# A new order of the tasks on all five engines in the steady part of a scan, mixture-of-experts and FFN kernel

## The chip, the cores and the metric

One core of one Trainium2 chip. The metric is the device time of one execution in microseconds (us); less is better. The engines are TensorE (PE in the rows, its weight loads PEld), VectorE (DVE), ScalarE (ACT), GpSimd (POOL) and SyncE (SP), which here only issues DMAs.

## The reference, cut to what matters

The input is x of shape (8, 1024, 128). Per sequence there is a selective state space scan with 16 states, then a top-1 mixture of 4 experts, two layer norms, and a gated FFN with a last layer norm:

```python
delta = softplus(x @ Wd + bd);  B = x @ WB + bB;  C = x @ WC + bC;  A = -exp(A_log)
# over time, for each of the 16 states s:
h = clip(exp(min(delta*A[s], 2)) * h + clip(delta*B[s], -2, 2) * x, -100, 100)
y = sum_s(h * C[s]) + x * D_param
routing = softmax(y @ Wr + br); top1
moe = (silu(y @ up_w[e] + up_b[e]) @ down_w[e] + down_b[e]) * top1_w
x1 = layernorm(x + layernorm(y + moe) * ln_w + ln_b)
out = layernorm(x1 + (silu(x1 @ w_gate.T) * (x1 @ w_up.T)) @ w_down.T)
```

## The kernel before

Each of the 8 sequences is a chunk (0 to 7) of 1024 tokens, in two halves of 512. The work of a chunk is cut into tasks; a task is a few instructions of one engine, written in the function `run` of that engine, and it waits by itself on semaphores for what it needs. In which order an engine takes the tasks stands in lists: `PE_ORDER`, `ACT_ORDER`, `DVE_ORDER`, `POOL_ORDER`, `SP_ORDER`. An entry such as `(-1, "up", 3)` is the task `up 3` of the chunk that is one behind the iteration's own. Each list is run through once an iteration, so three chunks are at work at a time: the scan of chunk n, the preparation of chunk n+1, the experts of chunk n-1 and the norms and the FFN of chunk n-2. The `_LAST` lists say in which order the last two chunks' tails are done. Every engine works strictly in its order: a task that waits holds all tasks behind it.

The tasks that matter here:

- Preparation: `z`, `bc` (TensorE) and their copies and `softplus` (ScalarE), `delta`, `dx` (VectorE), `b_turn`, `b_spread h` (TensorE, into PSUM bank T), `b_max`, `bound h` (VectorE, empties bank T), `over`, `flag`: a bound on whether clipping can happen at all. `bc_rest` and `bound_input` are GpSimd's part, `bc_mid`, `widen` and `x_scaled` ScalarE's, `bc_low` VectorE's.
- Scan, for each state s of 0 to 15: `decay s` (ScalarE, L807, exp), `spread s h` (TensorE, L555, B to all partitions into psB), `scan s` (VectorE: two multiplications by dx at L1209, two scans at L1218), `c s` (SP, a DMA of C to all partitions, L458), `prod s` (GpSimd, L1245), `add s` (TensorE, L561, transposed and summed in psY), and `skip` for the D term. Rings limit how far they run apart: 6 decays, 3 states, 3 products, 3 C tiles. `spread s+1` of a half needs `scan s` of this half; `scan s` needs `prod s-3`; `prod s` needs `add s-3`; the DMA `c s` needs `prod s-3`.
- Routing: `y_copy`, `yT_turn`, `yT_copy`, `logits`, `router_shift`, `rank`, `slots`, `router_exp`, `router_pick`, then `scatter 0` to `7` (GpSimd, L1266, indirect DMAs of the tokens to their expert's rows), `rows` (SP, L492), `sort_turn`, `sort_copy`.
- Experts, for 11 blocks k of 128 rows: `weights k` (SP, L486, 514 KB, a ring of 3, so it needs `result k-3`), `up k` (TensorE, L691, banks U0, U1 in turn), `silu k` (ScalarE, L846), `down k` (TensorE, L705, bank T), `result k` (ScalarE, L854); then `store` (SP) and `gather 0` to `7` (GpSimd, L1274).
- Norms and FFN, by halves h: `combine h` (VectorE, L1134), `stats h k` (L1152, L1157), `rstd h k` (GpSimd, L1283 to L1297), `centre h` (L1167), `affine h` (L1181), `x_shift h` (GpSimd, L1306), `norm h k` (ScalarE, L867), `x_turn h` (TensorE, L715, bank D), `x_high`, `x_rest`, `x_low`, `ff_up h 0` to `5` (banks U0, U1), `gate h m` (ScalarE, L904, silu), `ff_mul h m` (VectorE, L1189), `ff_down h`, `ff_part h m` (TensorE, L741, L585, bank D). `norm h 2` empties bank D.

ScalarE holds one table of functions at a time: exp, ln and silu each ask for a table load when another one is in place. Copies and scalings do not.

## Time and profile before

| | |
|---|---|
| time, median of 3 runs | 922.79 us (919.44 to 923.1) |
| span of the profiled execution (first to last instruction) | 920.4 us |
| VectorE busy | 715.4 us (78%) |
| TensorE matmuls busy / weight loads | 640.0 us / 511.3 us |
| GpSimd busy | 566.2 us |
| ScalarE busy | 537.6 us |

The times are of whole executions; for the profiled one there is its span alone, 2.4 us under the median. A busy share is an average over stages. The rows further down show what each engine did in stretches cut at the start of scan 0 of each chunk (33.98, 103.19, 193.43, 292.77, 392.77, 492.17, 590.83 and 690.68 us for chunks 0 to 7; the last scan ends at 788.53). Chunk 3 is the one whose timelines are shown.

### The profile page before, as it was taken

Reading aid. Unit: us, or ns where it says so; the run is one execution under the profiler, and the core shown is the slowest. Engines: PE = TensorE matmul, PEld = TensorE weight load, DVE = VectorE, ACT = ScalarE, POOL = GpSimd, SP = SyncE. Lnnn points to the kernel's source line nnn. Section 1 sums busy time; section 2 is a strip of 40 time slices with the busy share of each in tenths; the row PEclk is TensorE's granted clock in tenths of the full one; section 3 lists DMA queues with packets and bytes.
Section 4 is the critical chain, followed back from the end, with each engine's and each line's share of the span. In section 5 each row is a group of like instructions: output and inputs, shape, how many; then the busy total and the mean of one; then the engine's idle time right before and its main releaser. Section 6 shows DMA issues by size and latency. Waiting matters only on the chain.

```text
span 920.4 us, 14199 instructions
## 1 busy us (share of the span) xinstructions
PE 640.0 (70%) x4263; PEld 511.3 (56%) x4322; DVE 715.4 (78%) x1458; ACT 537.6 (58%) x988; POOL 566.2 (62%) x452
## 2 busy tenths in 40 slices
...
GB/s 102 128 127 115 138 149 148 243 225 189 112 218 237 197 96 190 239 166 153 163 243 202 188 113 219 247 203 85 203 240 138 156 166 247 89 82 154 135 23 24
DMA packets 82087, 149.31 MB, mean 162 GB/s; under 512 B 9404, under 2 KB 51144, under 8 KB 81992
## 3 DMA queue, kind: packets, MB, share of 16 engines
...
q8 instruction: 35, 0.57, 0.3%
...
## 4 chain that ended last, share of the span: by engine, by line
PE 30%; DVE 26%; issue 15%; ACT 15%; DMA 7%; POOL 4%; SPq 1%; another core or an unknown queue 0%; ACTq 0%; DVEq 0%; POOLq 0%
DVE state L1218 12%; DMA weights<-in_w_pack 5%; PE psY L561 4%; PE psU L691 4%; DVE psB L1209 4%; PE psD L585 4%; ACT hid L846 4%; PE psT L705 3%; ACT decay L807 3%; PE psU L732 2%; PE psU L734 2%; DVE bst L1152 2%; PE psB L555 2%; ACT L846 2%; PE psU L619 1%
## 5 line engine op out<-in xcount | busy, mean ns | idle before, releaser
L1245 POOL TENSOR_TENSOR prod<-state,c_wide 128x1024 f32<-128x1024 f32 x128 | 308.4, 2415 | 149.1 <-DVE state L1218 127.3
L1209 DVE TENSOR_TENSOR psB<-dx,psB 128x512 f32<-128x512 f32 x256 | 166.7, 689 | 31.6 <-PE psB L555 13.7
L1218 DVE TENSOR_TENSOR_SCAN state<-decay,state,psB 128x512 f32<-128x512 f32 x128 | 163.8, 1280 | 14.0
L555 PE MATMUL psB<-parts,sel 128*128 128x512 bf16 x198 | 89.5, 466 | 122.4 <-DVE state L1218 121.1
L1218 DVE TENSOR_TENSOR_SCAN state<-decay,psB 128x512 f32<-128x512 f32 x128 | 155.4, 1214 | 3.2 <-ACT decay L807 3.2
L561 PE MATMUL psY<-ident,prod 128*128 128x128 f32 x1024 | 155.0, 305 | 1.1 <-DVE state L1218 0.5
L807 ACT ACTIVATE decay<-delta,a_sb 128x1024 f32<-128x1024 f32 x128 | 142.0, 1141 | 15.7 <-DVE state L1218 7.4
L561 PEld LDWEIGHTS psY<-ident,prod 128*128 128x128 f32 x1024 | 137.5, 159 | 12.3 <-issue 7.9
L555 PEld LDWEIGHTS psB<-parts,sel 128*128 128x128 bf16 x256 | 25.8, 103 | 174.2 <-DVE state L1218 168.1
L846 ACT ACTIVATE hid<-psU,weights 128x128 f32<-128x128 f32 x352 | 99.7, 371 | 39.2 <-PE psU L691 33.7
L691 PE MATMUL psU<-yT_sorted,weights 128*128 128x128 f32 x704 | 96.1, 282 | 19.4 <-DMA weights<-in_w_pack 8.3
L691 PEld LDWEIGHTS psU<-yT_sorted,weights 128*128 128x128 f32 x704 | 86.8, 193 | 29.1 <-issue 15.6
L867 ACT ACTIVATE attn<-attn,shift,rstd 128x128 f32<-128x128 f32 x64 | 26.3, 481 | 124.8 <-POOL shift L1297 124.7
L705 PE MATMUL psT<-weights,hid 128*128 128x128 f32 x704 | 97.5, 281 | 0.0
L1266 POOL DMA_INDIRECT rows_in<-ytok,slot x64 | 66.1, 1033 | 44.2 <-issue 36.1
L705 PEld LDWEIGHTS psT<-weights,hid 128*128 128x128 f32 x704 | 85.8, 192 | 1.8
L1274 POOL DMA_INDIRECT chosen_out<-rows_out,slot x64 | 62.8, 981 | 22.7 <-issue 15.4
L1189 DVE SCALAR_TENSOR_TENSOR hh<-psU,hh 128x512 f32<-128x512 f32 x48 | 31.7, 682 | 40.8 <-PE psU L734 40.3
L854 ACT ACTIVATE result<-psT 128x128 f32<-128x128 f32 x88 | 24.7, 281 | 59.2 <-PE psT L705 57.3
L715 PE MATMUL psD<-ident,attn 128*128 128x128 f32 x60 | 13.3, 362 | 57.0 <-ACT attn L867 55.6
L1283 POOL TENSOR_TENSOR ve<-mv,eps 128x4 f32<-128x4 f32 x48 | 14.1, 294 | 59.8 <-DVE mv L1157 59.3
L585 PE MATMUL psD<-wdn_sb,hh 128*128 128x128 f32 x360 | 44.6, 275 | 0.4
...
## 6 DMA issues: line engine op xcount, KB each, us to landing
c_wide<-c_rows SPq DMA_DIRECT2D x128, 512.0 KB, 5.2
weights<-in_w_pack SPq DMA_DIRECT2D x88, 514.0 KB, 4.2
...
```

What stands on the lines that cost most here:

```text
L555: pe.matmul(tokens(psB, c, h), sel[:, s, :], parts[:, c.n % 2, h * HALF:h * HALF + c.hw], start=True, stop=True).then_inc(b_ready, 1)
L561: mm = pe.matmul(psY[:, j, :], src[:, j * ROWS:(j + 1) * ROWS], ident[:, :], is_transpose=True, start=(first and j % NJ == 0), stop=last, ...
L585: mm = pe.matmul(bank[d][:, cols], hh[:, m, cols], wdn_sb[:, m, :], start=False, stop=(m == NH - 1), skip_group_check=True)
L691: mm = pe.matmul(bank[u][:, f * ROWS:(f + 1) * ROWS], weights[:, q % NW, f * 128:(f + 1) * 128], yT_sorted[:, k * ROWS:(k + 1) * ROWS], st ...
L705: mm = pe.matmul(bank[d][:, 0:D], hid[:, k % 2, f, :], weights[:, q % NW, W_DOWN + f * D:W_DOWN + (f + 1) * D], start=False, stop=(f == NF ...
L807: nc.scalar.activation(decay[:, g % NDECAY, w], delta[:, n % 2, w], ACT.Exp, scale=a_sb[:, s:s + 1]).then_inc(decay_ready, 1)
L846: ins = nc.scalar.activation(hid[:, k % 2, f, :], bank[u][:, f * ROWS:(f + 1) * ROWS], ACT.Silu, bias=weights[:, q % NW, W_UPB + f:W_UPB + ...
L1209: v.tensor_tensor(tokens(psB, c, h), dx[:, n % 2, h * HALF:h * HALF + c.hw], tokens(psB, c, h), ALU.mult).then_inc(inp_ready, 1)
L1218: v.tensor_tensor_scan(state[:, g % NSTATE, t0:t0 + c.hw], decay[:, g % NDECAY, t0:t0 + c.hw], tokens(psB, c, h), before, ALU.mult, ALU.ad ...
L1245: g_.tensor_tensor(prod[:, g % NPROD, w], state[:, g % NSTATE, w], c_wide[:, g % NC, w], ALU.mult).then_inc(prod_ready, 1)
L1266: g_.indirect_dma_start(rows_in, bass.IndirectOffsetOnAxis(slot[:, n % 2, j:j + 1].bitcast(U32), 0), ytok[:, n % 2, j, :], None).then_inc( ...
L1274: g_.indirect_dma_start(chosen_out[:, j, :], None, rows_out, bass.IndirectOffsetOnAxis(slot[:, n % 2, j:j + 1].bitcast(U32), 0)).then_inc( ...
```

## The change

The five `_ORDER` lists and the `_LAST` lists are replaced. No task's own program, no tile and no semaphore is changed, and the tasks are the same ones. The new lists also begin their iteration at another place, which by itself does not change an engine's order; what follows is the order itself, read in the steady part for scan chunk n.

| engine | order before | order after |
|---|---|---|
| TensorE | yT_turn, spread 2, skip, logits | yT_turn, logits, spread 3, rank, skip |
| TensorE | x_turn 0, x_rest 0, add 4, ff_ups, b_turn | add 4, x_turn 0, b_turn, x_rest 0, ff_ups |
| TensorE | sort_turn 0, add 6, up 0, sort_turn 1, spread 10 0, up 1, spread 10 1 | add 7, sort_turn 0, spread 10 0, up 0, sort_turn 1, spread 10 1, up 1 |
| TensorE | spread 13 0, spread 13 1, x_turn 1, up 6, down 5 | spread 13 0, down 4, add 11, x_turn 1, up 6, spread 13 1 |
| TensorE | up 7, ff_up 1 2, spread 14 0, b_spread 1, ff_ups | up 7, b_spread 1, ff_up 1 2, ff_down 1, ff_ups, spread 14 0 |
| ScalarE | z_copy, bc_copy, decay 5, softplus, decays 6, 7, norm 0 1, x_high, decay 8, x_low, decay 9, gates, router_exp, decays 10, 11, 12 | z_copy, decays 4 to 10, bc_copy, decay 11, softplus, decay 12, norm 0 1, x_high, router_exp, x_low, gates, decay 13 |
| ScalarE | silu 9, silu 10, result 9, decay 0, result 10, decay 1 | silu 9, decay 0, result 8, silu 10, result 9, decay 1, result 10 |
| VectorE | combine 1, stats 1 0, centre 1, delta, scan 8; b_max, scan 9 | combine 1, delta, stats 1 0, scan 8; scan 9, b_max, scan 10, centre 1 |
| VectorE | scan 13, dx, bound 1, over, ff_mul 1 0, 1 1, router_pick | router_pick, dx, scan 13, bound 1, ff_mul 1 0, over, 1 1 |
| GpSimd | gathers 0 to 2, prod 1, 3 and 4, prod 2, scatter 0, prod 3, scatter 1, prod 4, x_shift 1, gathers 5 and 6, rstd 0 0, scatter 2, gather 7, scatter 3, rstd 0 1, scatter 4, prod 5, scatters 5 to 7 | gathers 0 to 3, prod 1, prod 2, gathers 4 to 6, prod 3, scatters 0 and 1, prod 4, scatter 2, rstd 0 0, prod 5, scatter 3, gather 7, rstd 0 1, scatters 4 to 7 |
| SP | weights 0, 1, 2, c 5, c 6, c 7, rows, c 8, c 9, c 10, weights 3, x | weights 0, c 5, c 6, weights 1, c 7, weights 2, c 8, rows, c 9, weights 3, c 10 |
| SP | weights 4, 5, c 11, c 12, weights 6, c 13 | weights 4, c 11, weights 5, x, weights 6, c 12, weights 7, c 13 |

The diff, cut to the lines that hold these places:

```diff
@@ -67,70 +67,68 @@
 PE_ORDER = [
-    (-1, "yT_turn"), (0, "spread", 2, 0), (0, "spread", 2, 1), (0, "skip"), (-1, "logits"), (0, "spread", 3, 0),
...
-    (0, "spread", 12, 1), (-1, "up", 5), (0, "add", 10), (-1, "down", 4), (0, "spread", 13, 0), (0, "spread", 13, 1),
-    (-2, "x_turn", 1), (-1, "up", 6), (-1, "down", 5), (-2, "x_rest", 1), (0, "add", 11), (-2, "ff_up", 1, 0),
...
+    (-2, "down", 4), (-1, "add", 11), (-3, "x_turn", 1), (-2, "up", 6), (-1, "spread", 13, 1), (-3, "x_rest", 1),
+    (-2, "down", 5), (-2, "warm"), (-3, "ff_up", 1, 0), (-3, "ff_up", 1, 1), (-2, "down", 6), (-2, "up", 7),
+    (0, "b_spread", 1), (-3, "ff_up", 1, 2), (-3, "ff_down", 1), (-3, "ff_up", 1, 3), (-3, "ff_up", 1, 4),
+    (-1, "spread", 14, 0), (-2, "down", 7), (-3, "ff_up", 1, 5), (-1, "spread", 14, 1), (-2, "up", 8),
...
 ACT_ORDER = [
-    (-2, "silu", 10), (-2, "result", 9), (0, "decay", 0), (-2, "result", 10), (-3, "norm", 1, 2), (0, "decay", 1),
...
-    (0, "decay", 5), (1, "softplus"), (0, "decay", 6), (0, "decay", 7), (-2, "norm", 0, 1), (-2, "x_high", 0),
-    (0, "decay", 8), (-2, "x_low", 0), (0, "decay", 9), (-2, "gate", 0, 0), (-2, "gate", 0, 1), (-2, "gate", 0, 2),
...
+    (-1, "decay", 7), (-1, "decay", 8), (-1, "decay", 9), (-1, "decay", 10), (0, "bc_copy"), (-1, "decay", 11),
+    (0, "softplus"), (-1, "decay", 12), (-3, "norm", 0, 1), (-3, "x_high", 0), (-2, "router_exp"), (-3, "x_low", 0),
+    (-3, "gate", 0, 0), (-3, "gate", 0, 1), (-3, "gate", 0, 2), (-1, "decay", 13), (-2, "sort_copy", 0),
...
+    (-2, "silu", 8), (-2, "silu", 9), (0, "decay", 0), (-2, "result", 8), (-2, "silu", 10), (-2, "result", 9),
+    (0, "decay", 1), (-2, "result", 10), (-3, "norm", 1, 2), (-1, "y_copy"), (0, "decay", 2), (-1, "yT_copy"),
...
 POOL_ORDER = [
-    (-2, "gather", 5), (-2, "gather", 6), (-2, "rstd", 0, 0), (-1, "scatter", 2), (-2, "gather", 7),
-    (-1, "scatter", 3), (-2, "rstd", 0, 1), (-1, "scatter", 4), (0, "prod", 5), (-1, "scatter", 5),
...
+    (-5, "gather", 6), (-3, "prod", 3), (-4, "scatter", 0), (-4, "scatter", 1), (-3, "prod", 4), (-4, "scatter", 2),
+    (-5, "rstd", 0, 0), (-3, "prod", 5), (-4, "scatter", 3), (-5, "gather", 7), (-5, "rstd", 0, 1),
+    (-4, "scatter", 4), (-4, "scatter", 5), (-4, "scatter", 6), (-4, "scatter", 7), (-3, "prod", 6), (-3, "prod", 7),
...
 PE_LAST = [
-    (-1, "ff_up", 0, 3), (-1, "ff_up", 0, 4), (-1, "ff_down", 0), (-1, "ff_up", 0, 5), (-1, "ff_part", 0, 0),
-    (-1, "ff_part", 0, 1), (-1, "ff_part", 0, 2), (-1, "x_turn", 1), (-1, "x_rest", 1), (-1, "ff_up", 1, 0),
+    (-1, "ff_up", 0, 3), (-1, "ff_down", 0), (-1, "ff_up", 0, 4), (-1, "ff_part", 0, 0), (-1, "ff_up", 0, 5),
+    (-1, "x_turn", 1), (-1, "ff_part", 0, 1), (-1, "x_rest", 1), (-1, "ff_part", 0, 2), (-1, "ff_up", 1, 0),
```

## Rows read from the trace of the kernel before

**Rows 1.** The page's first part: busy us, share of the span and instructions of each engine.
```profile
PE 640.0 (70%) x4263; PEld 511.3 (56%) x4322; DVE 715.4 (78%) x1458; ACT 537.6 (58%) x988; POOL 566.2 (62%) x452
```

**Rows 2.** Windows, scan 0 to scan 0: busy PE, PEld, DVE, ACT, POOL; clock; DMA.
```profile
103.19:193.43 90.24, 65.40 (x424) 53.73 (x432) 73.65 (x113) 50.69 (x93) 53.27 (x28) 0.82 0.57 186
193.43:292.77 99.34, 75.23 (x529) 61.49 (x537) 87.96 (x178) 66.67 (x121) 70.87 (x57) 0.86 0.57 186
292.77:392.77 100.00, 75.47 (x530) 61.49 (x538) 88.33 (x179) 68.02 (x125) 70.84 (x57) 0.88 0.58 184
...
590.83:690.68 99.85, 75.00 (x529) 61.40 (x536) 88.04 (x178) 68.08 (x125) 70.84 (x56) 0.88 0.58 187
690.68:788.53 97.85, 71.78 (x504) 60.13 (x512) 81.24 (x163) 54.63 (x111) 64.90 (x54) 0.84 0.53 173
788.53:920.40 131.87, 78.00 (x495) 60.96 (x493) 41.11 (x177) 47.74 (x122) 47.82 (x68) 0.79 0.28 83
```

**Rows 3.** VectorE's waits in chunk 3, 292.77 to 392.77: total us, times, longest.
```profile
DVE holder L1043 <- PE psT L637: 4.9, 2, 4.1
DVE psB L1209 <- PE psB L555: 2.2, 3, 0.9
...
DVE state L1218 <- ACT decay L807: 0.5, 1, 0.5
```

**Rows 4.** The page's costliest groups, one of them: busy us, mean ns, idle before.
```profile
L1218 DVE TENSOR_TENSOR_SCAN state<-decay,state,psB 128x512 f32<-128x512 f32 x128 | 163.8, 1280 | 14.0
```

**Rows 5.** Timeline of VectorE, chunk 3 and (411.96) 4: start us, us, instruction, idle before.
```profile
332.72 3.16 DVE L1134 SCALAR_TENSOR_TENSOR moe<-chosen_out,top_w,ytok 128x128 f32<-128x128 f32 x4
...
339.54 1.29 DVE L1209 TENSOR_TENSOR psB<-dx,psB 128x512 f32<-128x512 f32 x2
...
373.95 1.20 DVE L1030 TENSOR_TENSOR dx<-delta,xT_sb 128x1024 f32<-128x1024 f32 x1
379.27 0.06 DVE L1043 MEMSET holder<- 128x1 f32 x1 [4.11 <-PE psT L637]
...
411.96 1.14 DVE L1134 SCALAR_TENSOR_TENSOR moe<-chosen_out,top_w,ytok 128x128 f32<-128x128 f32 x4
```

**Rows 6.** Timeline of GpSimd in chunk 3: prod 5 and prod 13.
```profile
332.52 2.35 POOL L1245 TENSOR_TENSOR prod<-state,c_wide 128x1024 f32<-128x1024 f32 x1
...
374.12 3.25 POOL L1245 TENSOR_TENSOR prod<-state,c_wide 128x1024 f32<-128x1024 f32 x1 [1.18 <-DVE state L1218]
```

**Rows 7.** Timeline of ScalarE in chunk 3: norm 0 1, gates, norm 0 2.
```profile
331.01 1.65 ACT L867 ACTIVATE attn<-attn,shift,rstd 128x128 f32<-128x128 f32 x4 [12.31 <-POOL shift L1297]
...
338.01 1.28 ACT L904 ACT_TABLE_LOAD   x1
339.31 1.08 ACT L904 ACTIVATE hh<-psU 128x512 f32<-128x512 f32 x2
...
368.32 1.53 ACT L867 ACTIVATE x<-psD,shift,rstd 128x128 f32<-128x128 f32 x4
```

**Rows 8.** Timeline of TensorE's weight loads in chunk 3: up 5, x_turn 1, b_spread 1.
```profile
366.94 0.97 PEld L691 LDWEIGHTS psU<-yT_sorted,weights 128*128 128x128 f32 x8 [1.41 <-DMA weights<-in_w_pack]
...
370.03 0.57 PEld L715 LDWEIGHTS psD<-ident,attn 128*128 128x128 f32 x4
...
378.43 0.43 PEld L637 LDWEIGHTS psT<-identb,bmax 128*128 128x128 bf16 x4
```

**Rows 9.** The page's DMA issues: KB each, median us to landing.
```profile
weights<-in_w_pack SPq DMA_DIRECT2D x88, 514.0 KB, 4.2
```

**Rows 10.** Timeline of GpSimd in the tail: x_shift 1, scatter 2, scatter 7.
```profile
805.26 1.27 POOL L1306 TENSOR_TENSOR xt<-xt,lnb_sb 128x512 f32<-128x512 f32 x1
...
812.66 1.05 POOL L1266 DMA_INDIRECT rows_in<-ytok,slot  x1 [2.28 <-issue]
...
822.74 0.97 POOL L1266 DMA_INDIRECT rows_in<-ytok,slot  x1 [0.30 <-issue]
```

**Rows 11.** Timeline of TensorE in the last chunk's FFN: x_turn 1.
```profile
902.46 0.47 PEld L715 LDWEIGHTS psT<-ident,attn 128*128 128x128 f32 x4
```

More of the change, by code:

```diff
@@ L85 @@
[L85 to L88 removed]
+    (0, "b_spread", 0), (-1, "add", 8), (-1, "spread", 12, 0), (-1, "add", 9), (-3, "ff_part", 0, 2),
@@ new lines @@
+    (-3, "ff_part", 1, 0), (-2, "up", 9), (-3, "ff_part", 1, 1), (-3, "ff_part", 1, 2), (-2, "down", 8),
+    (-1, "spread", 15, 0), (-1, "spread", 15, 1), (-1, "add", 12), (-2, "up", 10), (-2, "down", 9),
+    (0, "spread", 0, 0), (-1, "add", 13), (0, "spread", 0, 1), (-2, "down", 10), (-1, "add", 14), (0, "spread", 1, 0),
+    (-1, "add", 15), (0, "spread", 1, 1), (1, "z"), (0, "spread", 2, 0), (-1, "yT_turn"), (0, "spread", 2, 1),
+    (-1, "logits"), (0, "spread", 3, 0), (0, "spread", 3, 1), (-1, "rank"), (0, "skip"), (0, "spread", 4, 0),
```

94 lines of the change are left out of this document (42 added, 52 removed), and 7 rows, old and new, of the table SP_ORDER.

## The prediction

> **What bounds the kernel now.** I read the busy shares first, then the same shares cut at each chunk's scan 0, then what VectorE waited for within one chunk, and last the timelines of all engines over that chunk. No engine is full over the whole span [rows 1]. Cut by chunk, VectorE is busy 88.3 of 100.0 us in chunk 3 and 88.0 of 99.9 in chunk 6; chunks 2 to 6, five such periods, add up to 497.3 us (193.43 to 690.68). TensorE's weight loads take 61.5 of 100 [rows 2]. So the steady part hangs on VectorE, with about 12 us a chunk in which it does nothing. Of those, 7.6 have a name: 4.9 waiting for `b_spread` ahead of `bound`, 2.2 for `spread`, 0.5 for a decay [rows 3]. The rest (some 4 us) is steps between instructions of 0.03 to 0.26 us; no order removes them all, and I leave 3.3 standing. A `scan` task is two multiplications, 1.29 us together [rows 5], and two scans of 1.28 or a little less [rows 4], which gives 3.8; sixteen take 61 us. VectorE's work is thus one fixed pile. An order can win named waits, one slow row (below), the ramp and the tail, and nothing more.
>
> From here "+40" is 40 us after the chunk's scan 0 starts. Before, a chunk has two halves: to about +50 VectorE runs without a hole, while TensorE, ScalarE and GpSimd have slack (ScalarE idles 12.3 us ahead of the norm at 331.01, +38.2 [rows 7]); from +50 to +100 TensorE is nearly full, VectorE waits for it.
>
> **What the change moves, and what each is worth.** No instruction is added but table loads. Per steady chunk, by engine:
>
> (a) GpSimd: prod 5 goes ahead of scatter 3, gathers 2 to 6 go ahead, both x_shifts go behind prod 12 and 14. Before, prod 5 starts at 332.52, 0.20 us ahead of combine 1 [rows 6]; that combine takes 3.16 us [rows 5] where the one at 411.96 takes 1.14 [rows 5]. In the new order GpSimd by then does rstd 0 1 (it still ends at +38.2) and four scatters; prod 5, free since scan 5 ends at +29.1, is over by +32.6. Combine 1 at +40.0 then costs 1.14: 2.0 us a chunk, on VectorE's path. The Trainium skill, "SBUF — State Buffer", Who interferes with whom, has the rule: a VectorE instruction with two SBUF inputs and a GpSimd one that reads SBUF exclude each other, the first to issue holding out the other. The row agrees; by a rule of shared bandwidth both would stretch, and prod took its usual 2.35.
>
> (b) VectorE: centre 1 goes from before scan 8 to behind scan 10, b_max behind scan 9, dx and router_pick ahead of scan 13. A move within a full stretch costs nothing; it lets scans 8 to 10 and the FFN multiplications start 1.1 us sooner. With (a): scan 8 at +43.7 instead of +46.8 (339.54 [rows 5]).
>
> (c) ScalarE: decays 8 to 12 and softplus move into the 12.3 us hole ahead of norm 0 1 (decay 12 needs scan 6, which ends at +33.8; its end is then +37.5, the norm's start +38.2, so nothing is late). bc_copy waits behind decay 10 and ends at +28; its readers come at +41. Gate 0 0 comes at +44.3 instead of +46.5 (339.31 [rows 7]), since decay 9 no longer stands between x_low and it. router_exp comes before the gates. Silu 0 comes at +52.8 instead of +56.4.
>
> (d) Table loads: exp, ln and silu each need their own. Read off the two lists, a chunk has 8 switches before and 10 after. Six only change their place; the two new ones come from silu 10, which now stands between decays 0 and 1. A switch is 1.28 us, 1.3 to the next start (338.01 to 339.31 [rows 7]), so 2.6 to 2.9 us more of ScalarE per chunk. At the chunk's end: decay 0 done +92.7, silu 10 +95.6, decay 1 +98.4; scan 1 asks for decay 1 at +100.1. Hidden by 1.7 us; if that cover is gone it costs 1 for 1. And decay 0 no longer comes late: 0.5 won [rows 3].
>
> (e) TensorE: add 4 and b_turn come earlier, skip after logits, spreads 10 and 11 ahead of the expert matmuls, b_spread 1 ahead of the last ff_ups. I walked the list on with durations of the rows (up 0.97, b_spread 0.43, x_turn 0.57 [rows 8]; down and add, 9 and 8 weight loads like up's 8, at 1.0 and 0.9; a hand-over between engines at 0.1 to 0.3): bound 0 starts at +65.8 (before: +70.3) with no wait for b_spread, scan 12 at +68.5 (+73.2), norm 0 2 ends at +73.3 (+77.1, from 368.32 plus 1.53 [rows 7]). Then new waits begin. Spread 13's second half now stands behind x_turn 1 and up 6. Weights 6 are asked for when result 3 is out, +69.3, and land 5 us after issue (median 4.2 [rows 9], and a C load joins), so up 6 runs at +75.1, the spread at +76.1, and scan 13 loses 2.0. Bound 1 waits for result 6 (+80.7) and b_spread 1: 2.5 lost, against 4.11 before [rows 5]. The multiplications behind lose 0.9, spreads 11 and 12 together 0.7. VectorE's waits: 6.1 instead of 7.6.
>
> (f) SP: c 10 now stands behind weights 3, c 12 behind weights 6, c 4 behind prod 1, which is behind four gathers. Each waiting DMA holds those behind it. Prod 12 so starts at +76 and ends at +78.4; scan 15 is the first to need it, at +92.4: 14 us of cover. Prod 10: +68.2 against scan 13 at +73.9, 5.7 of cover. And the late c 12 keeps prod 12 off dx (+72.7), which otherwise collide as in (a): before, dx at 373.95 [rows 5] pushed prod 13 to 3.25 us [rows 6]; if prod came first, dx would pay up to 2.3. Cost nothing, range 0 to 2.3.
>
> Sum per chunk: +96.2 by the walk, less the 0.5 of (d) that the first scan no longer waits: 95.7, of which 88.3 - 2.0 is work, 6.1 waits, 3.3 steps. Against 99.45 (497.3 / 5) that is 3.8 us, five times: 19. Bounds of the period: if only (a) holds, 97.4; if (e)'s waits all vanish, 89.6, of which I keep half, 92.6.
>
> **Ramp and tail.** Chunk 1 (90.2 us, VectorE 73.7 busy [rows 2]) waits at scans 9 to 12 for prod 6 and for spreads behind `up`; prod 5 earlier and the spreads ahead give 3.5 (between 0 and 6). Chunk 0 nothing. Chunk 7 (97.85) wins 2.0 from (a) and about 1 more: 3. In the tail, 131.9 us long [rows 2], the chain is slots, scatters 0 to 7, rows, experts. Before, x_shift 1 (1.27) and two gathers (1.3 each) stand in the midst of the scatters and GpSimd sits 2.28 before scatter 2; the last scatter starts at 822.74 [rows 10]. The new order has gathers 5 and 6 done before the slots are ready and x_shift before that: 3.9 less. Whether the 2.28 also go I can't tell; I take 4 (3.8 to 5.9). The experts (some 40 us) I leave as they are. In the last chunk's FFN, x_turn 1 at 902.46 [rows 11] stood behind ff_part 0 0 to 0 2 and now stands behind one of them: 2 (0 to 2.5). Tail: 6.
>
> Total 19 + 3.5 + 3 + 6 = 31.5 off the profiled execution's 920.4, 888.9. The median of the three runs shown, 922.79, lies 2.4 above that span; off the median it is 891.3.
>
> **Rivals.**
> Half the gain: the walk overlooks a wait of 2 to 2.5 us per chunk (dx against a prod, say). For: two of the covers above are under 2 us. Against: dx and prod 12 are 3 us apart. Time: 891.3 + 6 x 2.4 = 906.
> The two new table loads are on the path: 2.9 more per chunk, seven chunks, 891 + 20 = 911. Against: 1.7 us of cover at decay 1. The Trainium skill, "ScalarE: Activation LUTs", What ACT_TABLE_LOAD costs, adds a drain of 1.38 us to the 1.28 of every switch. By it the two extra would be 5.3 us a chunk and the time, my estimate from that page, 928, a little slower than before. The trace shows the next start 1.30 after the load's [rows 7], so no such drain here: 2 in 100, counted with the slower ones.
> Slower: the second half of spread 13, behind x_turn 1. That one waits for norm 0 2; before, both halves stood ahead of it (370.03 [rows 8]), so that the norm's lateness cost VectorE little. Now each us that the norm is later than +73.3 is a us of scan 13. 3.8 us eat the steady gain, from 6.3 on the kernel is slower; at 7.5 (rstd 0 2 stuck behind bound_input, rstd 1 1 and prod 10 because x_scaled is late) a chunk takes 103.2: 922.8 + 5 x 3.75 - 3.5 - 3 - 6 = 929.
> No change: gains in the steady part eaten fully, only some of the tail left: 919.
>
> **Chances.** Forecast 0.68 (its own range 880 to 900); half the gain 0.12; table loads on the path 0.05; no change within 0.5% (4.6 us, about what three runs can tell from nothing) 0.06; slower 0.09. The forecast's own case is 891. Leaving out the slower case, the no-change case and 5 in 100 at the low end: 878 (a period of 92.6 gives 891 - 5 x 3.1 = 876) to 912. Faster 0.85, same 0.06, slower 0.09.
>
> **What would show it.** Right: scan 0 to scan 0 at 95 to 97; combine 1 at 1.14 us in every chunk; 70 table loads instead of 58; a VectorE wait of about 2 us in the midst of scan 13, one of 2.5 before bound 1; the tail's last scatter 16 to 17 us after scatter 0's slots instead of 20. Wrong, if: combine 1 stays at 3.16, dx or centre 1 grows past 1.3, scan 1 waits for decay 1, the gap ahead of bound 1 stays at 4, or prod 12 holds up scan 15.

## The result, and the profile after

The changed kernel takes 911.94 us (median of 4 runs, 910.26 to 914.84) against 922.94 for the kernel before beside it; the ratio is 0.989, 95% interval 0.987 to 0.992. It is faster, by 11 us, where 31.5 were forecast. The profiled execution took 914.84 us, its span is 913.0. One of the eleven executions of the kernel before beside experiments 1, 2, 5 and 8 took 1057.18 us at a granted clock of 0.611 instead of about 0.83; their bracketed median of 924.4 holds it, the ratios leave it out. The page's first part (busy us, share, instructions of each engine):

```profile
PE 656.4 (72%) x4256; PEld 535.3 (59%) x4322; DVE 730.1 (80%) x1458; ACT 553.4 (61%) x1000; POOL 559.5 (61%) x452
```

VectorE does the same 1458 instructions and is busy 14.7 us longer than before [rows 1]. That is the first sign: its work is a fixed pile, so something on it got slower. The same windows as in [rows 2], cut at the new starts of scan 0 (chunks 1, 2, 4, 6, 7 and the tail):

```profile
106.35:191.13 84.78, 61.68 (x423) 51.45 (x431) 73.44 (x113) 52.71 (x92) 52.77 (x28) 0.86 0.59 201
191.13:290.75 99.62, 77.47 (x534) 64.13 (x541) 91.28 (x180) 70.69 (x128) 70.00 (x56) 0.86 0.55 184
...
388.87:488.82 99.95, 78.34 (x528) 64.65 (x537) 91.53 (x179) 70.51 (x127) 69.91 (x56) 0.85 0.57 184
...
586.86:686.98 100.12, 78.61 (x529) 64.67 (x537) 91.61 (x180) 70.76 (x127) 69.97 (x56) 0.85 0.55 184
686.98:787.45 100.47, 72.45 (x491) 61.03 (x500) 84.94 (x163) 53.04 (x107) 64.73 (x54) 0.85 0.53 172
787.45:913.01 125.56, 79.29 (x499) 64.15 (x498) 39.54 (x176) 48.34 (x127) 46.25 (x67) 0.76 0.29 87
```

Chunks 2 to 6 take 495.9 us (191.13 to 686.98) instead of 497.3: the steady part, where 19 were forecast, gave 1.4. VectorE is busy 91.5 in chunk 4, not the 86.3 of the forecast. The waits of VectorE in chunk 4, against those of [rows 3] (total us, times, longest):

```profile
DVE hh L1186 <- PE psU L731: 1.9, 4, 0.8
DVE holder L1040 <- PE psT L634: 1.9, 1, 1.9
DVE psB L1206 <- remote: 1.0, 1, 1.0
DVE psB L1206 <- issue: 0.3, 1, 0.3
```

So the waits did fall, to 5.1 us. Before they were 8.2: the 7.6 that the prediction read from [rows 3], and a row of 0.6 ("remote", ahead of L1209) that isn't among the lines shown there. The forecast was 6.1. What took their place stands in no list of waits; it is a long bar. Timelines of VectorE and GpSimd, chunk 4, from scan 2's end (all lines after the lists are 3 lower than before: L1065 is L1068, L1131 is L1134, L1206 is L1209, L1242 is L1245):

```profile
399.99 0.17 DVE L1060 TENSOR_TENSOR rs<-psT,br_sb 128x32 f32<-128x32 f32 x1
...
400.49 4.34 DVE L1065 TENSOR_TENSOR rs<-rs,rsmall 128x32 f32<-128x32 f32 x1
404.86 0.19 DVE L1069 SCALAR_TENSOR_TENSOR rcode<-rs,rev_sb 128x32 f32<-128x32 f32 x1
...
410.97 3.11 DVE L1131 SCALAR_TENSOR_TENSOR moe<-chosen_out,top_w,ytok 128x128 f32<-128x128 f32 x4
...
433.68 1.17 DVE L1131 SCALAR_TENSOR_TENSOR moe<-chosen_out,top_w,ytok 128x128 f32<-128x128 f32 x4
```

```profile
400.11 4.66 POOL L1242 TENSOR_TENSOR prod<-state,c_wide 128x1024 f32<-128x1024 f32 x2
...
410.80 2.35 POOL L1242 TENSOR_TENSOR prod<-state,c_wide 128x1024 f32<-128x1024 f32 x1 [2.40 <-PE psY L558]
```

The subtraction of `router_shift` works on 128x32 elements and takes 0.19 us when it is alone. Here it starts at 400.49, while prod 1 and prod 2 run back to back from 400.11 to 404.77, and ends at 404.83, just behind them. Combine 1, at 433.68, takes 1.17 us as forecast, but combine 0, at 410.97, starts 0.17 us behind prod 3 and takes 3.11. In the windows of chunks 2 to 7 the whole task `router_shift` takes 5.5 us instead of 1.4 to 1.6; combine 0 is long in four of them (2, 4, 6 and 7), 2.98 to 3.23 us instead of 1.14.

### The profile page after: what moved, and what is told of

Same layout as the page of the kernel before. It is cut to its first block, busy times and chain, and to the rows that moved or that the text cites. A ratio compares the mean times of both kernels' runs of the same rounds, so it can differ in the third digit from the quotient of the medians.

```text
span 913.0 us, 14204 instructions
## 1 busy us (share of the span) xinstructions
PE 656.4 (72%) x4256; PEld 535.3 (59%) x4322; DVE 730.1 (80%) x1458; ACT 553.4 (61%) x1000; POOL 559.5 (61%) x452
## 4 chain that ended last, share of the span: by engine, by line
DVE 35%; PE 25%; issue 18%; ACT 9%; POOL 7%; DMA 3%; SPq 1%; DVEq 1%; ACTq 0%; POOLq 0%; another core or an unknown queue 0%
DVE state L1215 14%; DVE psB L1206 6%; PE psT L702 4%; PE psU L688 3%; PE psU L731 3%; DVE rs L1065 3%; DVE bst L1149 3%; PE psU L729 3%; PE psD L582 2%; ACT hid L843 2%; PE psY L558 2%; POOL prod L1242 2%; DVE attn L1178 2%; ACT x L864 1%; ACT attn L864 1%
## 5 line engine op out<-in xcount | busy, mean ns | idle before, releaser
L1242 POOL TENSOR_TENSOR prod<-state,c_wide 128x1024 f32<-128x1024 f32 x128 | 303.0, 2376 | 160.0 <-DVE state L1215 109.2
L804 ACT ACTIVATE decay<-delta,a_sb 128x1024 f32<-128x1024 f32 x128 | 142.8, 1145 | 108.5 <-DVE state L1215 106.9
L1206 DVE TENSOR_TENSOR psB<-dx,psB 128x512 f32<-128x512 f32 x256 | 166.1, 688 | 20.8 <-remote 10.4
L1215 DVE TENSOR_TENSOR_SCAN state<-decay,state,psB 128x512 f32<-128x512 f32 x128 | 163.8, 1280 | 14.4 <-DVE state L1215 0.5
L552 PE MATMUL psB<-parts,sel 128*128 128x512 bf16 x191 | 86.1, 454 | 121.5 <-DVE state L1215 118.0
L558 PE MATMUL psY<-ident,prod 128*128 128x128 f32 x1024 | 161.6, 313 | 5.6 <-POOL prod L1242 2.6
L558 PEld LDWEIGHTS psY<-ident,prod 128*128 128x128 f32 x1024 | 146.4, 166 | 20.0 <-issue 10.2
L1263 POOL DMA_INDIRECT rows_in<-ytok,slot x64 | 69.5, 1086 | 21.0 <-issue 21.0
L1280 POOL TENSOR_TENSOR ve<-mv,eps 128x4 f32<-128x4 f32 x48 | 9.7, 201 | 71.2 <-DVE mv L1154 70.8
L582 PEld LDWEIGHTS psD<-wdn_sb,hh 128*128 128x128 f32 x360 | 43.5, 192 | 0.2
```

What stands on the lines that cost most here:

```text
L552: pe.matmul(tokens(psB, c, h), sel[:, s, :], parts[:, c.n % 2, h * HALF:h * HALF + c.hw], start=True, stop=True).then_inc(b_ready, 1)
L558: mm = pe.matmul(psY[:, j, :], src[:, j * ROWS:(j + 1) * ROWS], ident[:, :], is_transpose=True, start=(first and j % NJ == 0), stop=last, ...
L582: mm = pe.matmul(bank[d][:, cols], hh[:, m, cols], wdn_sb[:, m, :], start=False, stop=(m == NH - 1), skip_group_check=True)
L804: nc.scalar.activation(decay[:, g % NDECAY, w], delta[:, n % 2, w], ACT.Exp, scale=a_sb[:, s:s + 1]).then_inc(decay_ready, 1)
L1206: v.tensor_tensor(tokens(psB, c, h), dx[:, n % 2, h * HALF:h * HALF + c.hw], tokens(psB, c, h), ALU.mult).then_inc(inp_ready, 1)
L1215: v.tensor_tensor_scan(state[:, g % NSTATE, t0:t0 + c.hw], decay[:, g % NDECAY, t0:t0 + c.hw], tokens(psB, c, h), before, ALU.mult, ALU.ad ...
```

## The experiments

Times are medians, in brackets beside the kernel before on the same chip; "caught" means that a VectorE instruction was stretched beside a GpSimd product. Chunk n is always the window from scan 0 of chunk n on. The diffs are cut, some within a line, to the tasks that moved; experiment 2's and 3's leave out the lines of the semaphores and of the other operands.

**1. One task moved: prod 1 away from router_shift.**

```diff
-    (-5, "gather", 2), (-5, "gather", 3), (-3, "prod", 1), (-3, "prod", 2), (-5, "gather", 4),
+    (-5, "gather", 2), (-5, "gather", 3), (-3, "prod", 2), (-5, "gather", 4),
...
-    (-3, "prod", 14), (-4, "x_shift", 1), (-5, "rstd", 1, 2), (-3, "prod", 15), (-2, "prod", 0), (-4, "gather", 0),
-    (-4, "gather", 1),
+    (-3, "prod", 14), (-4, "x_shift", 1), (-5, "rstd", 1, 2), (-3, "prod", 15), (-2, "prod", 0), (-4, "gather", 0),
+    (-2, "prod", 1), (-4, "gather", 1),
```

> The changed kernel with one task moved: prod 1 goes from behind gather 3 to behind gather 0, so that two gathers and more lie between prod 1 and prod 2. Theory of the lock: in the changed kernel the subtraction inside router_shift (two inputs in SBUF) takes 4.3 us instead of 0.19 because GpSimd runs prod 1 and prod 2 back to back beside it. Here it should take about 0.2, and combine 0, which met prod 3 in half of the chunks at 3.1 us, should take 1.14 everywhere; six chunks times 4.15 plus about 7 for combine 0 would be 31, of which I expect 20 to 28: 884 to 892, period from scan 0 to scan 0 94 to 96. Rival (the steady part is held elsewhere: TensorE, the late half of spread 13, the two table loads): the subtraction gets short but the period stays above 97.5 and the time above 905, the time going to longer waits ahead of bound and in the midst of scan 13.

Measured: 887.3 us (924.4), ratio 0.961 (0.958 to 0.965). Timeline of VectorE, then of GpSimd, chunk 4:

```profile
391.27 0.17 DVE L1060 TENSOR_TENSOR rs<-psT,br_sb 128x32 f32<-128x32 f32 x1
...
391.76 0.19 DVE L1065 TENSOR_TENSOR rs<-rs,rsmall 128x32 f32<-128x32 f32 x1
```

```profile
387.75 2.35 POOL L1242 TENSOR_TENSOR prod<-state,c_wide 128x1024 f32<-128x1024 f32 x1
...
393.75 2.37 POOL L1242 TENSOR_TENSOR prod<-state,c_wide 128x1024 f32<-128x1024 f32 x1
```

Prod 1 (387.75) is over before the task, prod 2 (393.75) starts after it, and the subtraction takes 0.19. Combine 0 takes 1.14 to 1.16 in every chunk, too. The windows of chunks 3 and 4 show periods of 94.2 and 93.9 with VectorE busy 85.4:

```profile
285.90:380.10 94.20, 77.27 (x529) 64.47 (x537) 85.41 (x179) 70.61 (x127) 69.98 (x56) 0.89 0.60 196
380.10:474.00 93.90, 78.22 (x529) 64.94 (x537) 85.47 (x179) 70.55 (x127) 70.11 (x56) 0.87 0.59 196
```

In the changed kernel the five steady chunks took 25.4 us more than here (495.9 against 470.5), and the two tasks account for 26.5: `router_shift` took 5.45 to 5.54 instead of 1.35 to 1.38 in each of the five, 20.7 together, and combine 0 1.84, 1.97 and 1.98 more in three of them, 5.8. VectorE's waits in chunk 4 are, row for row, those shown above, so the time didn't go to other waits: the rival falls. The profiled execution is the fastest of six here (879.66); the whole spans differ by 35.1 (913.0 and 877.9), the medians by 24.6.

**2. The subtraction's input moved to PSUM, orders kept.** The addition writes bank T back, and maximum and subtraction read it there.

```diff
-                    v.tensor_tensor(rs[:, j, :], rs[:, j, :], wide(rsmall[:, 0, j], c.tiles, E), ALU.subtract
+                    v.tensor_tensor(rs[:, j, :], psr, wide(rsmall[:, 0, j], c.tiles, E), ALU.subtract
```

> The changed kernel with all its orders, but router_shift keeps its biased logits in PSUM: the addition writes bank T back, maximum and subtraction read bank T, so that the subtraction has one input in SBUF and one in PSUM. Bank T comes free three small instructions later (0.6 us). Theory of the lock: prod 1 and prod 2 still run back to back beside it, and the subtraction takes about 0.2 us all the same; the time falls by 15 to 25 to 887 to 897 (combine 0 may still meet prod 3). Rival (the subtraction is slow because VectorE's and GpSimd's traffic compete for SBUF, or because it waits for something else, such as the result of the maximum): it still takes over 1 us, and the time stays within 5 us of 912.

Measured: 911.3 us (924.4), ratio 0.988 (0.983 to 0.992): no gain over the changed kernel. Timeline of VectorE, chunk 4:

```profile
401.01 0.19 DVE L1066 TENSOR_TENSOR rs<-psT,rsmall 128x32 f32<-128x32 f32 x1
401.35 4.00 DVE L1071 SCALAR_TENSOR_TENSOR rcode<-rs,rev_sb 128x32 f32<-128x32 f32 x1
```

I had the price right for the instruction and wrong for the task: the subtraction, in the midst of the products (400.63 to 405.29), now takes 0.19, and the next one with two inputs in SBUF takes 4.00.

**3. All of router_shift with at most one input in SBUF, orders kept.** Biased logits, shifted ones and codes stay in bank T; a copy to rs is added for ScalarE.

```diff
+                    v.tensor_copy(rs[:, j, :], psr).then_inc(router_steps, 2)
-                    v.scalar_tensor_tensor(out=rcode[:, j, :], in0=rs[:, j, :], scalar=0.0,
+                    v.scalar_tensor_tensor(out=psc, in0=psr, scalar=0.0,
...
-                    v.tensor_tensor(chosen[:, j, :], rcode[:, j, :], wide(rsmall[:, 1, j], c.tiles, E), ALU.is_equal
+                    v.tensor_tensor(chosen[:, j, :], psc, wide(rsmall[:, 1, j], c.tiles, E), ALU.is_equal
```

> The changed kernel with all its orders; now every instruction of router_shift between the addition and chosen has at most one input in SBUF: the biased logits, the shifted ones and the codes stay in bank T, one small copy to rs is added for ScalarE. In the run that moved only the subtraction's input, the subtraction took 0.19 us and the next instruction with two SBUF inputs (rcode) took 4.00: the hold-up went to the next one in line. Theory of the lock: with none left, prod 1 and prod 2 still run back to back (4.66 us together) and router_shift takes about 1.6 us; nothing else holds, so the time falls by 20 to 28 to 884 to 892, the same as with prod 1 moved. Rival (VectorE is slowed by any GpSimd work beside it, or the later release of bank T costs TensorE as much): 900 or more, with some instruction of router_shift still above 1 us.

Measured: 899.6 us (921.8), ratio 0.976 (0.973 to 0.979). Timelines of GpSimd and VectorE, chunk 4:

```profile
397.42 4.67 POOL L1248 TENSOR_TENSOR prod<-state,c_wide 128x1024 f32<-128x1024 f32 x2
```

```profile
397.72 0.20 DVE L1067 TENSOR_TENSOR psT<-psT,rsmall 128x32 f32<-128x32 f32 x1
...
398.13 0.19 DVE L1072 SCALAR_TENSOR_TENSOR psT<-psT,rev_sb 128x32 f32<-128x32 f32 x1
...
398.58 0.19 DVE L1078 TENSOR_TENSOR chosen<-psT,rsmall 128x32 bf16<-128x32 f32 x1
399.22 1.29 DVE L1212 TENSOR_TENSOR psB<-dx,psB 128x512 f32<-128x512 f32 x2 [0.45 <-DVE chosen L1078]
...
404.66 3.96 DVE L1137 SCALAR_TENSOR_TENSOR moe<-chosen_out,top_w,ytok 128x128 f32<-128x128 f32 x4
```

The two products run over the whole task, and none of its instructions takes more than 0.20 us. The orders and the arithmetic are kept (a small copy and three semaphore steps come on top), so VectorE isn't slowed by GpSimd's work as such. The time, 899.6, misses my 884 to 892, and fell by half of what I expected, because combine 0 now comes to stand beside prod 3 (3.96 here), and a hand-over of 0.45 was added.

**4. A pause between the two products:** gather 4 goes in between.

```diff
-    (-5, "gather", 2), (-5, "gather", 3), (-3, "prod", 1), (-3, "prod", 2), (-5, "gather", 4),
+    (-5, "gather", 2), (-5, "gather", 3), (-3, "prod", 1), (-5, "gather", 4), (-3, "prod", 2),
```

> The changed kernel with gather 4 moved in between prod 1 and prod 2, so that about 1.2 us in which GpSimd reads no SBUF by its vector units lie between the two products; prod 1 still starts where router_shift's subtraction comes. Theory 1 (the subtraction is held as long as GpSimd goes from one such instruction straight to the next, and gets in at the first pause): it takes 2.0 to 2.3 us instead of 4.34, router_shift 3.2 to 3.5, 2.3 a chunk less, six chunks: 914 - 12 = 898 to 902. Theory 2 (held for the number of products that GpSimd has queued, or until its queue is empty): still over 4 us, 908 to 914. Theory 3 (a fixed wait of about 4 us): the same as theory 2 in time, with exactly 4.3.

Measured: 911.4 us (920.5), ratio 0.992 (0.989 to 0.995). Timelines of VectorE and GpSimd, chunk 4:

```profile
401.39 2.05 DVE L1065 TENSOR_TENSOR rs<-rs,rsmall 128x32 f32<-128x32 f32 x1
...
403.92 3.04 DVE L1075 TENSOR_TENSOR chosen<-rcode,rsmall 128x32 bf16<-128x32 f32 x1
```

```profile
401.02 2.36 POOL L1242 TENSOR_TENSOR prod<-state,c_wide 128x1024 f32<-128x1024 f32 x1
403.54 0.98 POOL L1271 DMA_INDIRECT chosen_out<-rows_out,slot  x1 [0.16 <-issue]
404.55 2.35 POOL L1242 TENSOR_TENSOR prod<-state,c_wide 128x1024 f32<-128x1024 f32 x1
```

Theory 1 holds for the instruction: held by prod 1 alone, the subtraction takes 2.05 us and gets in at the pause. But the time didn't follow, because the task's last instruction has two inputs in SBUF as well; it is ready at 403.92 and ends at 406.96, behind prod 2 (404.55 to 406.90). Its start is put 0.6 us ahead of prod 2's, in the midst of gather 4, and so it is in each of chunks 2 to 7 here.

The gather isn't what holds: over all runs 933 starts of such instructions (router_shift's three, combine, centre and affine) fall within a gather or scatter that has no instruction right behind it, and all take their usual 0.19 to 0.21 or 0.32 to 0.35 us. Of the 79 that start within one with a product right behind it, 29 are held through that product. Their starts lie 0.16 to 0.71 us ahead of the product's; of the 50 that aren't held, 45 start 0.71 to 1.06 ahead. So it isn't enough to start first by the trace: within some 0.7 us the product mostly wins. Whether it took the ports before its start in the trace, or the start of VectorE's instruction isn't its grant, stays open.

**5. My part (a) alone, in the kernel before:** prod 5 ahead of scatter 3.

```diff
-    (-1, "scatter", 3), (-2, "rstd", 0, 1), (-1, "scatter", 4), (0, "prod", 5), (-1, "scatter", 5),
+    (0, "prod", 5), (-1, "scatter", 3), (-2, "rstd", 0, 1), (-1, "scatter", 4), (-1, "scatter", 5),
```

> The kernel before with one task moved: prod 5 goes from behind scatter 4 to ahead of scatter 3. My part (a) alone. By my prediction combine 1 falls from 3.16 to 1.14 in the chunks where it was long, 2.0 us a chunk, 7 chunks: 909 to 913. Rival (VectorE's slack is decided behind +50 by TensorE, and what is won at combine 1 is waited away at bound 0 or at spreads 11 to 13): combine 1 gets short, the waits for b_spread and spread grow by as much, and the time stays above 918.

Measured: 939.1 us (924.4), ratio 1.017 (1.012 to 1.021). Neither theory: the time lies above the rival's 918, but not by the rival's mechanism. Timelines of VectorE and GpSimd, chunk 3:

```profile
326.74 3.97 DVE L1181 SCALAR_TENSOR_TENSOR attn<-moe,rstd,xt 128x128 f32<-128x128 f32 x4
...
335.79 1.12 DVE L1134 SCALAR_TENSOR_TENSOR moe<-chosen_out,top_w,ytok 128x128 f32<-128x128 f32 x4
...
342.33 1.30 DVE L1209 TENSOR_TENSOR psB<-dx,psB 128x512 f32<-128x512 f32 x2 [1.65 <-PE psB L555]
```

```profile
327.68 2.35 POOL L1245 TENSOR_TENSOR prod<-state,c_wide 128x1024 f32<-128x1024 f32 x1
```

Combine 1 is short, but prod 5 now falls on `affine 0`, which takes 3.97 us instead of 1.12. And the 2.0 won behind it aren't kept: affine 0 feeds norm 0 1, the gates and, through TensorE's order, spread 8, for which VectorE now waits 1.65. The period of chunk 3 grows by as much as affine 0, 2.8 (102.8 instead of 100.0).

**6. GpSimd's new steady list in the kernel before, all else as before.** Its core:

```diff
-    (-2, "gather", 0), (-2, "gather", 1), (-2, "gather", 2), (0, "prod", 1), (-2, "gather", 3), (-2, "gather", 4),
-    (0, "prod", 2), (-1, "scatter", 0), (0, "prod", 3), (-1, "scatter", 1), (0, "prod", 4), (-2, "x_shift", 1),
...
+    (-5, "gather", 2), (-5, "gather", 3), (-3, "prod", 1), (-3, "prod", 2), (-5, "gather", 4), (-5, "gather", 5),
+    (-5, "gather", 6), (-3, "prod", 3), (-4, "scatter", 0), (-4, "scatter", 1), (-3, "prod", 4), (-4, "scatter", 2),
```

> The kernel before with GpSimd's steady list of the changed kernel, all other lists as before. By the lock theory prod 1 and prod 2 now run back to back just when scan 2 ends and router_shift begins: its subtraction grows from 0.2 to 0.5 us to about 4.3, six chunks, plus 24. Combine 1 gets short (2.0 us a chunk), but the run with prod 5 moved alone showed that lateness of norm 0 1 is passed on whole and that scan 8 then waits for its spread; so I count little for it: 935 to 948. Rival, the sum of my prediction (combine 1 counts in full, and four less in the scatters): 905 to 915.

Measured: 970.1 us (921.8), ratio 1.052 (1.048 to 1.055), beyond even my 935 to 948. Timelines of VectorE and GpSimd, chunk 3:

```profile
352.75 6.34 DVE L1167 SCALAR_TENSOR_TENSOR moe<-moe,mv,lnw_sb 128x128 f32<-128x128 f32 x4
```

```profile
353.72 4.69 POOL L1245 TENSOR_TENSOR prod<-state,c_wide 128x1024 f32<-128x1024 f32 x2
```

In chunk 3 `router_shift` takes 5.22 (before 1.63), combine 0 1.81 (1.15), centre 0 3.20 (1.12), combine 1 1.17 (3.16), and centre 1, caught by prod 6 and prod 7 in a row, 6.34 (1.14): 3.6 + 0.7 + 2.1 - 2.0 + 5.2 = 9.6, of which shorter waits give back 0.7 (7.5 instead of 8.2): the period is 108.5 instead of 100.0. The list that is good with the new VectorE order costs 48 us with the old one. My sum had treated (a) as a property of GpSimd's list.

**7. Part (a) undone inside experiment 1:** prod 5 back behind scatter 4.

```diff
-    (-5, "rstd", 0, 0), (-3, "prod", 5), (-4, "scatter", 3), (-5, "gather", 7), (-5, "rstd", 0, 1),
-    (-4, "scatter", 4), (-4, "scatter", 5),
+    (-5, "rstd", 0, 0), (-4, "scatter", 3), (-5, "gather", 7), (-5, "rstd", 0, 1),
+    (-4, "scatter", 4), (-3, "prod", 5), (-4, "scatter", 5),
```

> The changed kernel with prod 1 behind gather 0 (887.3 us) and prod 5 put back behind scatter 4, which undoes my part (a) inside the new order. Prod 5 then starts about 0.2 us ahead of combine 1, which should take 3.0 to 3.2 us again instead of 1.14. Theory A (part (a) as predicted, 2.0 us a chunk on VectorE's path): 899 to 902. Theory B (VectorE waits 1.24 us ahead of ff_mul 0 0 for ScalarE's gates, which hang on affine 0 and norm 0 1, not on combine 1; the delay is taken up by that wait and the 0.1 to 0.3 behind it): 0.5 us a chunk, 889 to 893.

Measured: 893.6 us (921.8), ratio 0.971 (0.968 to 0.973), between the theories. Timeline of VectorE, chunk 3:

```profile
326.27 3.17 DVE L1131 SCALAR_TENSOR_TENSOR moe<-chosen_out,top_w,ytok 128x128 f32<-128x128 f32 x4
...
335.54 1.26 DVE L1186 SCALAR_TENSOR_TENSOR hh<-psU,hh 128x512 f32<-128x512 f32 x2
```

Set beside experiment 1 from scan 0 on, combine 1 ends 2.1 us later, scan 9 0.6 later (the wait ahead of `ff_mul 0 0` took up the rest), then centre 1 is caught for 0.5 and bound 1 waits 0.3 longer: 1.35 at the end of the chunk. Part (a) is worth 1.35 a chunk in this order, not 2.0.

**8. Two table loads fewer:** silu 10 ahead of decay 0 again, in the changed kernel.

```diff
-    (-2, "silu", 8), (-2, "silu", 9), (0, "decay", 0), (-2, "result", 8), (-2, "silu", 10), (-2, "result", 9),
+    (-2, "silu", 8), (-2, "silu", 9), (-2, "silu", 10), (0, "decay", 0), (-2, "result", 8), (-2, "result", 9),
```

> The changed kernel with silu 10 put back ahead of decay 0, and so two table loads fewer a chunk (58 in all instead of 70). My prediction: the two loads are hidden, the time stays within 3 us of 912. Rival (they are on the path, 2.9 us a chunk): 892 to 900. Decay 0 comes some 3 us later here, so up to 0.5 a chunk may be lost at scan 0.

Measured: 946.5 us (924.4), ratio 1.027 (1.022 to 1.031), 35 us slower than the changed kernel and outside both theories. Timelines of ScalarE and VectorE, end of chunk 3:

```profile
396.29 1.14 ACT L843 ACTIVATE hid<-psU,weights 128x128 f32<-128x128 f32 x4 [3.85 <-PE psU L688]
...
398.74 1.15 ACT L804 ACTIVATE decay<-delta,a_sb 128x1024 f32<-128x1024 f32 x1
399.80 0.26 ACT L851 ACTIVATE result<-psT 128x128 f32<-128x128 f32 x1
```

```profile
401.54 0.69 DVE L1206 TENSOR_TENSOR psB<-dx,psB 128x512 f32<-128x512 f32 x1 [2.92 <-PE psB L552]
403.48 0.70 DVE L1206 TENSOR_TENSOR psB<-dx,psB 128x512 f32<-128x512 f32 x1 [1.25 <-PE psB L552]
```

Silu 10 waits 3.85 us for up 10, which the new TensorE order has put late. Behind it stand decay 0 and result 8; down 9 needs result 8, and spread 0 stands behind down 9. VectorE waits 4.2 us for it. So the two extra loads buy something I had priced at 0.5: with this TensorE order decay 0 and result 8 can't stand behind silu 10. For the loads themselves the sign is in the changed kernel, where VectorE waits for decay 1 in no chunk; no run takes them out alone.

**9. Spread 13 in one piece, in experiment 1.**

```diff
-    (-2, "down", 4), (-1, "add", 11), (-3, "x_turn", 1), (-2, "up", 6), (-1, "spread", 13, 1), (-3, "x_rest", 1),
+    (-2, "down", 4), (-1, "spread", 13, 1), (-1, "add", 11), (-3, "x_turn", 1), (-2, "up", 6), (-3, "x_rest", 1),
```

> The changed kernel with prod 1 behind gather 0 (887.3 us in its run) and one more task moved: on TensorE the second half of spread 13 goes from behind up 6 to directly behind down 4, so that it no longer waits for x_turn 1 and up 6. My prediction's rival put a price of 1 for 1 on that place. Theory A (bound 1 waits for b_spread 1 behind up 7, so what scan 13 no longer waits, about 1.0 us a chunk, bound 1 waits longer): within 2 us of 887. Theory B (the wait in scan 13 is on the path): 6 to 8 us less, 879 to 881.

Measured: 886.1 us (921.8), ratio 0.962 (0.959 to 0.964), the same as experiment 1. VectorE's wait for b_spread 1 in chunk 3:

```profile
DVE holder L1040 <- PE psT L634: 2.8, 1, 2.8
```

The wait in the midst of scan 13 (0.8 in chunk 3 of experiment 1, 1.0 in chunk 4) is gone, bound 1 waits 2.8 instead of 1.9, and the multiplications behind it 1.9 instead of 2.4. Chunks 2 to 6 take 470.3 us, against 470.5. Theory A.

**10. That wait attacked: b_spread 1 ahead of down 6, in experiment 9.**

```diff
-    (-2, "down", 5), (-2, "warm"), (-3, "ff_up", 1, 0), (-3, "ff_up", 1, 1), (-2, "down", 6), (-2, "up", 7),
-    (0, "b_spread", 1), (-3, "ff_up", 1, 2),
+    (-2, "down", 5), (-2, "warm"), (-3, "ff_up", 1, 0), (-3, "ff_up", 1, 1), (0, "b_spread", 1), (-2, "down", 6),
+    (-2, "up", 7), (-3, "ff_up", 1, 2),
```

> The fastest order so far (prod 1 behind gather 0, spread 13 unparted, 886.1 us) with b_spread 1 moved on TensorE from behind up 7 to ahead of down 6. Bound 1 now waits 2.9 us a chunk for it. Theory A (that wait is on the path and can be had): 2 us a chunk less, six or seven chunks, 872 to 876. Theory B (TensorE is the bound between +70 and +90: down 6 now waits until bound 1 has emptied bank T, and VectorE waits as much longer for ff_up, for spread 14 or for decay 0): within 3 us of 886, or slower.

Measured: 900.5 us (920.5), ratio 0.977 (0.974 to 0.980). Timelines of VectorE and of TensorE's weight loads, chunk 3:

```profile
371.19 0.06 DVE L1040 MEMSET holder<- 128x1 f32 x1 [0.86 <-PE psT L634]
...
376.81 0.69 DVE L1186 SCALAR_TENSOR_TENSOR hh<-psU,hh 128x512 f32<-128x512 f32 x1 [4.27 <-PE psU L731]
```

```profile
372.59 0.10 PEld L699 LDWEIGHTS psT<-bias,of_block 96*128 96x128 bf16 x1 [1.81 <-DVE peak L1043]
```

Bound 1 waits 0.9 instead of 2.8, but down 6 waits 1.81 for bank T, and VectorE 4.27 for ff_up 1 3, which stands behind up 7 and ff_up 1 2. In this execution router_shift was caught in chunk 3 (4.17), but in chunks 4 to 6, with nothing caught, the period is 96.0 to 97.6 too, instead of 93.5 to 94.6 in experiment 9. Theory B: between +70 and +90 TensorE sets the pace.

**11. and 12. More cover for the last catches.** In experiment 9's profile chunk 7 was still caught, in router_shift (3.95) and in combine 0 (3.34). First scatter 0 goes ahead of prod 3 (experiment 11), then also gather 4 ahead of prod 2 (12); the diff shows both, against experiment 9.

```diff
-    (-5, "gather", 2), (-5, "gather", 3), (-3, "prod", 2), (-5, "gather", 4), (-5, "gather", 5),
-    (-5, "gather", 6), (-3, "prod", 3), (-4, "scatter", 0), (-4, "scatter", 1),
+    (-5, "gather", 2), (-5, "gather", 3), (-5, "gather", 4), (-3, "prod", 2), (-5, "gather", 5),
+    (-5, "gather", 6), (-4, "scatter", 0), (-3, "prod", 3), (-4, "scatter", 1),
```

> The same order as the fastest so far (886.1 us) with scatter 0 ahead of prod 3 on GpSimd. Scatter 0 waits for the slots, and combine 0 comes 0.1 us behind these, so prod 3 can't start before combine 0 any more, whatever else drifts. In the runs so far that used prod 1 behind gather 0, combine 0 or router_shift was still caught in one chunk (3.3 to 4.0 us). Expected: combine 0 at 1.14 in all chunks, 2 us less: 883 to 886. Rival: prod 3 later holds C loads and scatters, no gain: 886 to 889.

Measured: 884.7 us (920.5), ratio 0.960 (0.957 to 0.963). Combine 0 takes 1.14 in all chunks; router_shift is caught in two (4.13 and 4.15).

> The order with scatter 0 ahead of prod 3 (884.7 us) with gather 4 also moved ahead of prod 2. There router_shift was still caught by prod 2 in two chunks (4.1 us instead of 1.36): in these scan 2 or the logits came 0.5 to 0.9 us later than in the others, and between router_shift's end and prod 2 lie only 1.1 us. One gather more puts prod 2 at +14.8 and the cover at 2.3 us. Expected by the lock theory: router_shift 1.36 to 1.5 and combine 0 at 1.14 in every chunk, periods 93.5 to 94.5, 5 us less: 878 to 882. Rival: prod 2 comes 1.3 us later and holds prod 3, the scatters and the DMAs of C behind it; some scan waits for it and the time stays at 884 or more.

Measured: 883.8 us (922.6), ratio 0.958 (0.954 to 0.961), span of the profiled execution 879.1. No router_shift, combine, centre or affine is caught in any chunk, and the six steady periods from chunk 2 to 7 are 93.9 to 94.5; the window of chunk 3:

```profile
286.40:380.90 94.50, 77.44 (x529) 64.71 (x537) 85.32 (x180) 70.66 (x127) 70.05 (x56) 0.89 0.62 195
```

The intervals of experiments 1, 9, 11 and 12 overlap, so I rank none of them; each beats both kernels. Their runs still spread over 3 to 11 us (879 to 888 in the last). Only one execution of each was profiled: experiment 1's is its fastest (879.66), with nothing caught, experiment 11's its slowest (887.55), with two catches. That fits catches that come in some executions and not in others, but what makes the slower ones is open.

## Why the prediction was right in sign and wrong in size

**The step that failed** is the term for VectorE's work in the sum, "88.3 - 2.0 is work", with "VectorE's work is thus one fixed pile" and part (a) behind it: GpSimd's new order was priced only where its products meet combine 1 (and, in (f), dx), and at nothing everywhere else. The work measured 89.5 to 91.6 us in chunks 2 to 6, not 86.3. What the runs showed in its place: prod 1 and prod 2, now in a row at scan 2's end, hold `router_shift`'s subtraction for 4.3 to 4.4 us in every steady chunk, and prod 3 catches combine 0 in every other one. It costs 20.7 us in chunks 2 to 6 by router_shift and 5.8 us by combine 0, each against experiment 1. Experiment 6 gives the same catch of router_shift with VectorE's old order, so it is (a) that was wrong and not (b).

I had the rule and its price in hand: the Trainium skill, "SBUF — State Buffer", Who interferes with whom, says that any VectorE instruction with two SBUF inputs and a GpSimd instruction that reads SBUF exclude each other. The trace agrees (0.19 us alone, 4.34 beside two products; 0.19 beside them with one input in PSUM). What I didn't do is walk the rule over all such instructions of VectorE: router_shift, combine 0, centre 0 and affine 0 are of this kind too. That gathers 0 to 3 now stand ahead of prod 1 and none between it and prod 2 is written in the table of the change, and I passed over it. Before, gathers lay between prod 1 and prod 2, and router_shift took at most 0.3 us more than in experiment 1.

- **The rest of the sum foresaw too little gain, not too much.** Without the catches the period is 94.1 (470.5 / 5) against the 95.7 of my walk. The forecast of bound 0 at +65.8 and of scan 12 at +68.5 met +65.6 and +68.4 in chunk 3 of experiment 1. Of the sum's terms, work is 85.4 to 85.6 instead of 86.3, the waits are 5.1 in chunk 4 instead of 6.1 (scan 13 1.0 instead of 2.0, bound 1 1.9 instead of 2.5, but the multiplications behind it 1.9 instead of 0.9), and the steps, 3.3, are met (93.9 - 85.5 - 5.1).
- **(a)** Combine 1 fell to 1.12 to 1.17 as said. Its worth was overstated: 1.35 a chunk in the new order, and in the old one the gain was lost to affine 0 and to spread 8.
- **(d)** 70 table loads and no wait for decay 1, as forecast. That their place, with result 8, is worth about 5 a chunk to this TensorE order I had not seen; I had written 0.5.
- **(e)** The forecast's first half was right, and experiments 9 and 10 show why nothing more is to be had there by such moves: what scan 13 saves, bound 1 waits, and what bound 1 saves, ff_up takes.
- **(f)** Prod 12 met nothing: dx took 1.19 and 1.28 in chunks 3 and 4, and scan 15 of chunk 3 had no wait.
- **Ramp.** Chunk 1 won 5.5 (84.8 against 90.2), forecast 3.5; router_shift isn't caught in it (1.38). Chunk 0 lost 2.5, forecast 0: scans 6 and 9 wait 0.9 each for a spread, and scan 4 waits twice for 0.4.
- **Chunk 7** lost 2.6 where I had 3 won: scan 13 waits 2.7 in its midst there, and the stretch is one in which router_shift and combine 0 were caught as well.
- **Tail.** 125.56 instead of 131.87 [rows 2]: 6.3, forecast 6, but the parts differ, so that this agreement is in part luck. From scatter 0 to the last scatter it takes 15.1 us (818.90 - 803.84), where it took 19.8 (822.74 - 802.95): 4.7 won, 4 forecast. But scatter 0 starts 16.4 after the last scan's end (803.84 - 787.45) instead of 14.4, so that the last scatter is only 2.8 us earlier against that mark (31.5 instead of 34.2), and the last x_turn 6.4 (107.6 after it, 895.00 - 787.45; before 902.46 - 788.53 = 113.9 [rows 11]). In experiment 1, with nothing caught in chunk 7, scatter 0 starts 13.2 after the mark and the tail is 121.4 long (756.50 to 877.9): catches in chunk 7 seem to cost in the tail too, but no run tests that alone. Timeline of GpSimd in the tail of the changed kernel, scatters 0, 2 and 7:

```profile
803.84 1.00 POOL L1263 DMA_INDIRECT rows_in<-ytok,slot  x1 [2.57 <-issue]
...
807.38 0.98 POOL L1263 DMA_INDIRECT rows_in<-ytok,slot  x1 [1.26 <-issue]
...
818.90 0.97 POOL L1263 DMA_INDIRECT rows_in<-ytok,slot  x1 [0.30 <-issue]
```

The rival "half the gain: the walk overlooks a wait of 2 to 2.5 us per chunk (dx against a prod, say)" named the kind of cause, with the wrong instruction and half its size: a pair of products in a row holds twice as long, and its 906 was still 6 too low. That 911.9 falls on the 911 of the table-load rival, and just inside the 912 at the top of the range, is luck: VectorE waits for decay 1 in no chunk. The rival of the late spread 13 fell as well: experiment 9 takes its wait away and gains nothing.
